# A four-layer graph network on one core: row transposes as fp32r, reordered evictions, and six small loads on another queue

## The chip, the cores and the metric

One core of a Trainium2 chip. The metric is the device time of one launch, in microseconds, as the median of three runs. TensorE does the matrix products and writes to PSUM banks; VectorE and ScalarE read those banks; GpSimd works on SBUF only; the queues of SyncE and ScalarE issue DMAs.

## The reference

16 graphs of 1024 nodes with 256 features, and a dense matrix of 1024 x 1024 per graph. Four layers, each `x = layernorm(x + layer(x))`, all in float32:

- layer 0: five small graph convolutions over groups of the first 25 nodes of each graph;
- layer 1: attention, `softmax over (leaky(ai + aj) where adj > 0, and a sink)` times `z = x W + bW`, with `ai` and `aj` a dot product of `z` per node;
- layer 2: `relu(((1 + eps) x + adj x) W1 + b1) W2 + b2`, hidden width 512;
- layer 3: `silu(rmsnorm((eps x + adj x) W1 + b1)) W2 + b2`, hidden width 1024.

## The kernel before, in words

A prologue computes layer 0 for all graphs at once (lines 113 to 654), and the scores of graph 0; then one loop over the 16 graphs does layers 1 to 3. Products are made from high and low parts: `hi` is the fp32r rounding of a value and `lo` what is left, and three matmuls (hi hi, hi lo, lo hi) make one product. The order on each engine is written out by hand in one function per engine (`graph`), and semaphores tie the engines. Graph b+1's scores and attention are prepared inside graph b.

TensorE's order in graph b (function `graph` in the tensor block):

1. aggregation of layer 1, node columns 0 to 511 (half 0), k = 0 to 7: `agg_step`, six matmuls of 128x512 each (L950, L951, L954); with it the end of layer 3 of graph b-1;
2. half 1, k = 0 to 7; behind most steps `turn_col(k, h)`, four transposes (L915) of a tile of the adjacency's columns into one of two turn banks (banks 4 and 5, taken in turn); behind k = 2 `attention_out(b, 0)` (L980, 24 matmuls);
3. aggregation of layer 2: half 0, k = 0 to 3, with `attention_out(b, 1)` behind k = 1 and `turn_col(3, 1)`, `(4, 1)`, `(5, 1)` behind k = 1, 2, 3; half 1, k = 0 to 3, with `turn_col(6, 1)` and `(7, 1)`; then k = 4 to 7 of both halves, with `aj_rows` (L928: eight transposes of a broadcast column of `aj`, the row of scores) behind k = 6 of half 1;
4. layer 2's hidden tiles (`hidden_tile`, six matmuls, L1000, L1001, L1005) and second products (L1015, fp32), for half 0 and then half 1. Hidden tile n uses bank n mod 2 and waits until tile n-2 was read;
5. aggregation of layer 3; hidden tiles of layer 3, half 0 (m = 0 to 7), with `turn_att(b+1, k)` (L901: eight transposes of an attention tile, four into each turn bank) behind m = 0, m = 4 and m = 7; the end of half 1's aggregation around `rms_sum` (L1047); `rms_row` (L1059, four transposes of a broadcast column of `rms`); `turn_att(b+1, 3)`; then hidden tiles of half 1, each with the second product of half 0 (L1029, L1033).

Who empties the banks:

- ScalarE reads a turn bank into `mt_hi` (`turn_hi`, L1163, both halves of an attention tile; `turn_col_hi`, L1174), VectorE then writes `mt_lo` (`turn_lo`, L1497; `turn_col_lo`, L1503) and frees the bank.
- `relu(b, h, m)` (L1227, ScalarE) empties a hidden bank of layer 2; `leaky` (L1210) and `exp` (L1215) are the scores of graph b+1, and `score_mask` (L1579) and `scores` (L1585) are VectorE's part of them.
- `square(b, h, m)` (ScalarE, two instructions, L1237 and L1246) empties a hidden bank of layer 3, and `add_square` (VectorE, L1611) sums the squares.
- `statistics` (VectorE, L1543 and after), a power on GpSimd (L1375), `normalize` (VectorE, L1558), `x_high` (ScalarE, L1201), `x_low` (GpSimd, L1380) turn a residual sum (`residual`, L1526 and L1531) into the next layer's operands. `agg_hi` (ScalarE, L1191) and `agg_lo` (VectorE, L1515) make `a_hi` and `a_lo` from an aggregation bank.

In the prologue ScalarE's queue issues 17 DMAs (L232 to L251) ahead of its first computation, `fus_e` (L254), which VectorE waits for (L408) before it empties the banks with the transposed adjacency (`AT`, L456); ScalarE copies those side by side (`AT_side`, L265) in 28 pieces; TensorE's L580 waits for the last. SyncE's queue issues the graphs, layer 0's weights, x, four weight matrices (L215 to L218; VectorE's L415 waits for all four) and eight adjacency rows (L220).

Of the kernel before, what the change touches and what calls it, by code (L numbers as in the profile page):

```python
# [46 lines left out]
def adj_resnorm(nc, x, adj, L0_W1, L0_b1, L0_W2, L0_b2, L0_fusion_w, W, bW, wai, bai, waj, baj,  # L47
# [3 lines left out]
    with ExitStack() as ctx:  # L51
# [41 lines left out]
        ai, aj = sb("ai", [P, NT]), sb("aj", [P, NT])  # L93
# [5 lines left out]
        graph0 = (att, att_r, ident_r, x_even, sq_sum, stat0, mv0, ve, rstd, qi, qj, ai, aj)  # L99
# [14 lines left out]
def prologue(nc, ctx, sem, banks, ident, ones, WT_hi, WT_lo, W12, W12_hi, W12_lo, W13, W13_hi, W13_lo,  # L114
# [4 lines left out]
    att, att_r, ident_r, x_even, sq_sum, stat0, mv0, ve, rstd, qi, qj, ai, aj = graph0  # L119
# [6 lines left out]
    with ExitStack() as pro:  # L126
# [70 lines left out]
        with nc.Block() as block:  # L197
            @block.sync
            def _(sp):
# [30 lines left out]
            def _(act):  # L230
                with nc.allow_non_contiguous_dma(reason="small columns"):
# [13 lines left out]
                    for dst, src in ((b12[:], L2_b1.rearrange("(t p) -> p t", p=P)),  # L245
                                     (b13[:], L3_b1.rearrange("(t p) -> p t", p=P)),
                                     (rms_col[:], rms_w.rearrange("(t p) -> p t", p=P)),
                                     (bW_row[:], row(bW).to_broadcast([P, D])),
                                     (b22_row[:], row(L2_b2).to_broadcast([P, D])),
                                     (b23_row[:], row(L3_b2).to_broadcast([P, D]))):  # L250
                        act.dma_start(dst, src).then_inc(s_bload, 16)  # L251
# [4 lines left out]
                for g in range(NG):  # L256
# [5 lines left out]
                    for first, run in GROUP_RUNS[g]:  # L262
                        src = AT[:, g].rearrange("p t (b j) -> p t b j", j=PAD)
                        for t in range(T0):
                            last = nc.scalar.activation(cols[:, t, :, at:at + run], src[:, t, :, first:first + run], ACT.Copy)  # L265
                        at += run
# [390 lines left out]
def layers(nc, sb, sem, banks, ident, ones, WT_hi, WT_lo, W12_hi, W12_lo, W13_hi, W13_lo,  # L657
# [5 lines left out]
    att, att_r, ident_r, x_even, sq_sum, stat0, mv0, ve, rstd, qi, qj, ai, aj = graph0  # L663
# [33 lines left out]
    ms, rms = sb("ms", [P, 2, 4]), sb("rms", [P, 2, 4])  # L697
# [118 lines left out]
    with nc.Block() as block:  # L816
# [74 lines left out]
        def _(pe):  # L891
# [29 lines left out]
            def aj_rows(b, first):  # L921
                pe.wait_ge(s_aj, b + 1)
                for i in range(2):
                    if not first:
                        turn_free(i, turn_aj_use(b))
                    for j in HALF_TILES:
                        t = 4 * i + j
                        mm = nc.tensor.transpose(turn_bank[i][:, j * P:(j + 1) * P],  # L928
                                                 aj[:, t:t + 1].to_broadcast([P, P]), ident[:])
# [121 lines left out]
            def rms_row(b, h):  # L1051
# [107 lines left out]
        def _(act):  # L1159
            def turn_hi(b, k):  # L1160
                for i in range(2):
# [96 lines left out]
            def graph(b, buf, first, last):  # L1258
# [233 lines left out]
        def _(dve):  # L1492
            def turn_lo(b, k):
                for i in range(2):
# [135 lines left out]
            def graph(b, buf, first, last):  # L1630
# [165 lines left out]
```

## Time and profile before

| | |
|---|---|
| median of 3 runs | 2726.66 us (2725.57 to 2726.69) |
| the profiled execution | 2724.53 us, span 2722.7 us |
| granted TensorE clock, mean over the span | 0.984 |
| prologue, up to the first `aj_rows` | 97.4 us |
| one graph, from `aj_rows` to `aj_rows`, 1156.00 to 1316.88 | 160.9 us |
| TensorE busy in that graph | 158.8 us, granted clock 1.00 |
| VectorE, ScalarE, GpSimd busy in it | 124.9, 96.1, 78.5 us |

A row of a timeline reads: start, time from the start of the first to the end of the last of the instructions that are merged in it, engine, line, operation, output<-inputs, shape, count, and in brackets the idle time of the engine before it and what ended it. Matmuls are pipelined, so rows of TensorE overlap; the distance from one start to the next is what a matmul costs in a stream.

### The profile page before, as it was taken

What the parts mean: (1) busy time and instruction counts of PE and PEld (TensorE: products, weight loads), DVE (VectorE), ACT (ScalarE), POOL (GpSimd) and SP (SyncE); (2) the same over time, 40 slices, a digit from 0 to 9 for tenths busy, and PEclk for the clock granted to TensorE, in tenths of its full rate; (3) what the DMA queues carried; (4) which work ended last, traced back from release to release, by engine and by line L of the source; (5) the groups of instructions that cost most, each with busy time, mean ns of one, the idle gap of its engine ahead of it and who ended that gap; (6) DMA issues with size and microseconds to landing.
All of it is one profiled execution on the core that took longest, in us unless ns stands there. A gap on an engine that the chain in (4) does not pass through costs nothing.

```text
span 2722.7 us, 41123 instructions
## 1 busy us (share of the span) xinstructions
PE 2608.1 (96%) x14650; PEld 2229.5 (82%) x14650; DVE 2030.3 (75%) x4504; ACT 1557.8 (57%) x2911; POOL 1274.9 (47%) x1385
## 2 busy tenths in 40 slices
PE   6499999999999999999999999999999999999997
PEld 5478888888888888888888888888888888888886
DVE  5776877868787786868878686886878778687735
ACT  2546557564755756466575646656475675647524
POOL 2243554535455454545535454553535555354533
PEclk8699999999999999999999999999999999999998
DMA  7040402204040220403013040311304022040200
GB/s 227 20 126 1 155 1 82 74 10 146 1 147 10 77 79 1 155 1 122 34 47 109 1 155 1 95 61 30 126 1 155 1 86 71 12 144 1 78 1 16
DMA packets 205224, 181.00 MB, mean 66 GB/s; under 512 B 17367, under 2 KB 186718, under 8 KB 205022
## 3 DMA queue, kind: packets, MB, share of 16 engines
q1 hardware_dynamic: 197454, 177.04, 20.4%
q10 hardware_dynamic: 7568, 1.34, 0.4%
q8 instruction: 118, 1.93, 0.3%
q14 instruction: 84, 0.69, 0.1%
HBM read 161.15 MB, written 17.19 MB: 65 GB/s over the span
## 4 chain that ended last, share of the span: by engine, by line
PE 68%; DVE 16%; ACT 8%; issue 4%; POOL 1%; ACTq 0%; DVEq 0%; POOLq 0%
PE bank L950 10%; PE bank L954 9%; PE bank L951 9%; PE bank L1015 8%; PE bank L1000 6%; PE bank L1001 6%; PE bank L1005 6%; PE bank L1029 5%; PE bank L901 3%; DVE stat L1543 3%; PE bank L1033 2%; DVE x_odd L1558 2%; DVE x_even L1558 2%; DVE hid L1627 2%; ACT hid L1251 2%
## 5 line engine op out<-in xcount | busy, mean ns | idle before, releaser
L950 PE MATMUL bank<-mt_hi,x_hi 128*128 128x512 f32 x1536 | 627.5, 409 | 0.8 <-ACT x_hi L1201 0.7
L954 PE MATMUL bank<-mt_hi,x_lo 128*128 128x512 f32 x1536 | 602.2, 392 | 0.0
L951 PE MATMUL bank<-mt_lo,x_hi 128*128 128x512 f32 x1536 | 601.1, 391 | 0.0
L1375 POOL TENSOR_TENSOR rstd<-ve,neg_half 128x4 f32<-128x4 f32 x126 | 161.3, 1280 | 416.0 <-DVE ve L1551 415.6
L954 PEld LDWEIGHTS bank<-mt_hi,x_lo 128*128 128x128 f32 x1536 | 289.2, 188 | 62.9 <-POOL x_lo L1380 0.2
L950 PEld LDWEIGHTS bank<-mt_hi,x_hi 128*128 128x128 f32 x1536 | 289.3, 188 | 56.8 <-ACT scratch L1246 6.6
L951 PEld LDWEIGHTS bank<-mt_lo,x_hi 128*128 128x128 f32 x1536 | 290.2, 189 | 49.5
L1000 PE MATMUL bank<-a_hi,W_lo 128*128 128x512 f32 x768 | 316.8, 412 | 3.7 <-ACT hid L1227 2.9
L1611 DVE TENSOR_TENSOR sq_sum<-sq_sum,scratch 128x512 f32<-128x512 f32 x224 | 154.9, 691 | 216.0 <-ACT scratch L1246 216.0
L1001 PE MATMUL bank<-a_hi,W_hi 128*128 128x512 f32 x768 | 301.7, 393 | 0.0
L1029 PE MATMUL bank<-W_hi,hid_hi 128*128 128x256 f32 x1024 | 263.0, 290 | 19.8 <-ACT hid_hi L1256 19.8
L1174 ACT ACTIVATE mt_hi<-bank 128x512 fp32r<-128x512 f32 x256 | 153.0, 598 | 221.3 <-PE bank L915 221.3
L1029 PE MATMUL bank<-W_lo,hid_hi 128*128 128x256 f32 x1024 | 257.2, 284 | 0.0
L1237 ACT ACTIVATE hid<-bank,b 128x512 f32<-128x512 f32 x256 | 176.7, 690 | 133.5 <-PE bank L1033 77.5
L1515 DVE TENSOR_TENSOR a_lo<-bank,a_hi 128x512 fp32r<-128x512 f32 x192 | 126.2, 685 | 162.9 <-ACT a_hi L1191 162.7
L1251 ACT ACTIVATE hid<-hid 128x512 f32<-128x512 f32 x256 | 161.2, 630 | 146.3 <-DVE hid L1627 144.7
L1005 PE MATMUL bank<-a_lo,W_hi 128*128 128x512 f32 x768 | 237.9, 391 | 0.0
L1380 POOL TENSOR_TENSOR x_lo<-x_even,x_hi 128x256 fp32r<-128x256 f32 x192 | 162.7, 862 | 143.8 <-ACT x_hi L1201 143.8
L1503 DVE TENSOR_TENSOR mt_lo<-bank,mt_hi 128x512 fp32r<-128x512 f32 x256 | 173.1, 685 | 72.3 <-ACT mt_hi L1174 72.0
L1015 PE MATMUL bank<-W,hid 128*128 128x256 f32 x1024 | 226.2, 379 | 0.0
L1191 ACT ACTIVATE a_hi<-bank 128x512 fp32r<-128x512 f32 x192 | 109.0, 593 | 201.1 <-PE bank L954 197.1
L1029 PEld LDWEIGHTS bank<-W_hi,hid_hi 128*128 128x128 f32 x1024 | 195.2, 191 | 31.9 <-issue 26.6
(169 smaller groups left out, 5978.1 us busy)
## 6 DMA issues: line engine op xcount, KB each, us to landing
att<-in_adj SPq DMA_DIRECT2D x128, 512.0 KB, 8.1
adj_col<-in_adj SPq DMA_DIRECT2D x256, 256.0 KB, 3.0
out<-x_even SPq DMA_DIRECT2D x64, 128.0 KB, 2.9
out<-x_odd SPq DMA_DIRECT2D x64, 128.0 KB, 2.7
x_odd<-in_x SPq DMA_DIRECT2D x56, 128.0 KB, 4.2
x_even<-in_x SPq DMA_DIRECT2D x49, 128.0 KB, 3.8
G<-in_L_gnn_W SPq DMA_DIRECT2D x2, 2048.0 KB, 19.0
W_raw<-in_L_gnn_W SPq DMA_DIRECT2D x2, 1024.0 KB, 10.5
```

Source lines behind the costliest of these rows:

```text
L950: nc.tensor.matmul(dst[:], hi, mt_hi[:, k, cols], start=k == 0, stop=False)
L951: nc.tensor.matmul(dst[:], hi, mt_lo[:, k, cols], start=False, stop=False)
L954: mm = nc.tensor.matmul(dst[:], lo, mt_hi[:, k, cols], start=False, stop=done)
L1000: nc.tensor.matmul(dst, w_lo[:, d, cols], a_hi[:, d, :], start=d == 0, stop=False)
L1001: nc.tensor.matmul(dst, w_hi[:, d, cols], a_hi[:, d, :], start=False, stop=False)
L1005: mm = nc.tensor.matmul(dst, w_hi[:, d, cols], a_lo[:, d, :], start=False, stop=d == DT - 1)
L1015: mm = nc.tensor.matmul(out_bank[t // 2][:, t % 2 * D:(t % 2 + 1) * D], src[:, t * P:(t + 1) * P], W22[:, m, :], start=(m == 0 and t % 2 = ...
L1029: nc.tensor.matmul(out_bank[t // 2][:, t % 2 * D:(t % 2 + 1) * D], hi[:, t * P:(t + 1) * P], r[:, m, :], start=(m == 0 and t % 2 == 0 and ...
L1237: nc.scalar.activation(hid[:, m, :], src, ACT.Identity, bias=b13[:, m:m + 1])
L1251: nc.scalar.activation(h_m, h_m, ACT.Silu).then_inc(s_silu, 1)
L1380: nc.gpsimd.tensor_tensor(x_lo[:, t, :], x_bufs[buf][:, t, :], x_hi[:, t, :].bitcast(F32), ALU.subtract).then_inc(s_x_lo, 1)
L1503: nc.vector.tensor_tensor(mt_lo[:, k, cols], turn_bank[i][:], mt_hi[:, k, cols].bitcast(F32), ALU.subtract).then_inc(s_turn_free[i], 1)
```

## The change

- `aj_r` and `rms_r` are fp32r names for the memory of `aj` and `rms`; `aj_rows` and `rms_row` transpose these with `ident_r`, instead of the fp32 tiles with `ident`.
- ScalarE, layer 2: `relu(b, 0, m)` for m = 1, 2, 3 moves ahead of `leaky(b+1, m-1)`.
- VectorE, layer 1: `turn_col_lo(b, 4, 0)` moves ahead of `statistics(b+1, 0, 0)`; `turn_col_lo(b, 3, 1)` moves ahead of `residual(b, 1, 1)`.
- Layer 3, half 0: the two halves of attention tiles 0 and 1 are evicted apart: ScalarE's half 0 behind `square` 0 (and 4), half 1 behind `square` 1 (and 5); VectorE's half 0 behind `add_square` 1 (and 5), half 1 behind `add_square` 2 (and 6).
- TensorE: `turn_att(b+1, 3)` moves from ahead of hidden tile 0 of half 1 to behind it.
- Prologue: six loads of bias columns and rows move from ScalarE's queue to the end of SyncE's loads; the 28 copies of `AT_side` become 7, each over all four tiles.

```diff
+        with ExitStack() as place:
+            aj_r = sb("aj_r", [P, NT], F32R, place)
+        aj, ai = sb("aj", [P, NT]), sb("ai", [P, NT])
...
                 for t in range(NT):
                     sp.dma_start(att[:, t, :], adj[0, t * P:(t + 1) * P, :]).then_inc(s_att_in[t], 16)
+                with nc.allow_non_contiguous_dma(reason="small columns"):
+                    for dst, src in ((b12[:], ...), (b13[:], ...), (rms_col[:], ...),
+                                     (bW_row[:], ...), (b22_row[:], ...), (b23_row[:], ...)):
+                        sp.dma_start(dst, src).then_inc(s_bload, 16)
                 sp.wait_ge(s_bload, 16 * 6)
...
-                    for dst, src in ((b12[:], ...), ...):
-                        act.dma_start(dst, src).then_inc(s_bload, 16)
...
-                        for t in range(T0):
-                            last = nc.scalar.activation(cols[:, t, :, at:at + run], src[:, t, :, first:first + run], ACT.Copy)
+                        last = nc.scalar.activation(cols[:, :, :, at:at + run], src[:, :, :, first:first + run], ACT.Copy)
...
-                        mm = nc.tensor.transpose(turn_bank[i][:, j * P:(j + 1) * P],
-                                                 aj[:, t:t + 1].to_broadcast([P, P]), ident[:])
+                        mm = nc.tensor.transpose(turn_bank[i][:, j * P:(j + 1) * P].bitcast(F32R),
+                                                 aj_r[:, t:t + 1].to_broadcast([P, P]), ident_r[:])
...
-                    mm = nc.tensor.transpose(row_bank[:, j * P:(j + 1) * P],
-                                             rms[:, h, j:j + 1].to_broadcast([P, P]), ident[:])
+                    mm = nc.tensor.transpose(row_bank[:, j * P:(j + 1) * P].bitcast(F32R),
+                                             rms_r[:, h, j:j + 1].to_broadcast([P, P]), ident_r[:])
...
                 rms_row(b, 0)
-                if not last:
-                    turn_att(b + 1, 3)
                 for m in range(HT3):
                     hidden_tile(b, 3, 1, m)
+                    if not last and m == 0:
+                        turn_att(b + 1, 3)
...
                 diag_hi(b, 1)
+                relu(b, 0, 1)
                 if not last:
                     leaky(b + 1, 0)
-                relu(b, 0, 1)
+                relu(b, 0, 2)
                 if not last:
                     leaky(b + 1, 1)
-                relu(b, 0, 2)
+                relu(b, 0, 3)
                 if not last:
                     leaky(b + 1, 2)
-                relu(b, 0, 3)
-                if not last:
                     exp(b + 1, 0)
...
                     square(b, 0, m)
-                    if not last and m in (0, 4):
-                        turn_hi(b + 1, m // 4)
+                    if not last and m % 4 < 2:
+                        turn_hi(b + 1, m // 4, (m % 4,))
...
                 turn_col_lo(b, 3, 0)
+                turn_col_lo(b, 4, 0)
                 if not last:
                     statistics(b + 1, 0, 0, 1 - buf)
-                turn_col_lo(b, 4, 0)
                 turn_col_lo(b, 5, 0)
...
+                turn_col_lo(b, 3, 1)
                 residual(b, 1, 1, buf)
-                turn_col_lo(b, 3, 1)
                 turn_col_lo(b, 4, 1)
...
                     add_square(b, 0, m)
-                    if not last and m in (1, 5):
-                        turn_lo(b + 1, m // 4)
+                    if not last and m % 4 in (1, 2):
+                        turn_lo(b + 1, m // 4, (m % 4 - 1,))
```

## Rows read from the trace of the kernel before

**Rows 1.** The page, its first part: busy time and share of the span by engine.

```profile
PE 2608.1 (96%) x14650; PEld 2229.5 (82%) x14650; DVE 2030.3 (75%) x4504; ACT 1557.8 (57%) x2911; POOL 1274.9 (47%) x1385
```

**Rows 2.** Timeline of TensorE, layer 3 of a graph from the middle.

```profile
1210.45 0.80 PE L901 MATMUL bank<-ident_r,att_r 128*128 128x128 f32 x8
...
1212.08 0.62 PE L1005 MATMUL bank<-a_lo,W_hi 128*128 128x512 f32 x2
...
1214.10 0.50 PE L1000 MATMUL bank<-a_hi,W_lo 128*128 128x512 f32 x1
...
1215.60 0.97 PE L901 MATMUL bank<-ident_r,att_r 128*128 128x128 f32 x8
...
1223.94 0.35 PE L1029 MATMUL bank<-W_hi,hid_hi 128*128 128x256 f32 x1 [0.94 <-ACT hid_hi L1256]
```

**Rows 3.** Timeline of ScalarE, the squares of hidden tiles 5 and 6.

```profile
1212.76 0.71 ACT L1237 ACTIVATE hid<-bank,b 128x512 f32<-128x512 f32 x1
1213.33 0.71 ACT L1246 ACTIVATE scratch<-bank,b 128x512 f32<-128x512 f32 x1
1214.10 0.69 ACT L1237 ACTIVATE hid<-bank,b 128x512 f32<-128x512 f32 x1
```

**Rows 4.** Timeline of VectorE, the low parts of attention tile 1.

```profile
1214.69 1.28 DVE L1497 TENSOR_TENSOR mt_lo<-bank,mt_hi 128x512 fp32r<-128x512 f32 x2
```

**Rows 5.** Timeline of VectorE, layers 1 and 2 of the next graph.

```profile
1273.74 1.40 DVE L1543 BATCH_NORM_STATS2 stat<-x_even 128x6 f32<-128x256 f32 x4
...
1275.66 1.28 DVE L1503 TENSOR_TENSOR mt_lo<-bank,mt_hi 128x512 fp32r<-128x512 f32 x2
...
1292.13 1.28 DVE L1515 TENSOR_TENSOR a_lo<-bank,a_hi 128x512 fp32r<-128x512 f32 x2
...
1298.31 1.66 DVE L1526 SCALAR_TENSOR_TENSOR x_odd<-bank,rden,x_odd 128x256 f32<-128x256 f32 x4
...
1303.01 0.69 DVE L1503 TENSOR_TENSOR mt_lo<-bank,mt_hi 128x512 fp32r<-128x512 f32 x1
```

**Rows 6.** Timelines of ScalarE and of GpSimd, the same stretch.

```profile
1273.77 0.61 ACT L1174 ACTIVATE mt_hi<-bank 128x512 fp32r<-128x512 f32 x1
...
1306.78 2.98 POOL L1380 TENSOR_TENSOR x_lo<-x_odd,x_hi 128x256 fp32r<-128x256 f32 x4
```

**Rows 7.** Timeline of TensorE, the same stretch and its `aj_rows`.

```profile
1276.49 0.51 PE L915 MATMUL bank<-ident_r,mt_lo 128*128 128x128 f32 x4 [0.20 <-DVE mt_lo L1503]
...
1293.62 0.28 PE L980 MATMUL bank<-WT_hi,a_hi 128*128 128x256 f32 x1
...
1300.71 0.52 PE L915 MATMUL bank<-ident_r,mt_lo 128*128 128x128 f32 x4 [0.54 <-DVE mt_lo L1503]
...
1304.26 0.46 PE L915 MATMUL bank<-ident_r,mt_lo 128*128 128x128 f32 x4
...
1316.88 1.04 PE L928 MATMUL bank<-ident,aj 128*128 128x128 f32 x8
```

**Rows 8.** Timelines of ScalarE and TensorE, layer 2's hidden tiles.

```profile
1322.85 0.67 ACT L1227 ACTIVATE hid<-bank,b 128x512 f32<-128x512 f32 x1
...
1333.92 0.67 ACT L1227 ACTIVATE hid<-bank,b 128x512 f32<-128x512 f32 x1
...
1323.57 0.50 PE L1000 MATMUL bank<-a_hi,W_lo 128*128 128x512 f32 x1 [0.19 <-ACT hid L1227]
...
1334.70 0.43 PE L1000 MATMUL bank<-a_hi,W_lo 128*128 128x512 f32 x1
```

**Rows 9.** Timelines of ScalarE (and its queue), TensorE and VectorE in the prologue.

```profile
16.59 2.91 ACTq L251 DMA_DIRECT2D b<-in_L_gnn_b  x2
...
29.59 1.28 ACT L254 ACT_TABLE_LOAD   x1 [29.59 <-issue]
...
36.43 4.65 PE L580 MATMUL bank<-AT_side,X 128*128 128x212 f32 x16 [6.89 <-ACT AT_side L265]
...
49.50 0.69 DVE L415 CAST W_hi<-W_raw 128x1024 fp32r<-128x1024 f32 x1 [4.39 <-DMA W<-in_L_gnn_W]
```

More of the change, by code:

```diff
@@ L92, in adj_resnorm @@
         qi, qj = sb("qi", [P, NT]), sb("qj", [P, NT])
-        ai, aj = sb("ai", [P, NT]), sb("aj", [P, NT])
+        with ExitStack() as place:
+            aj_r = sb("aj_r", [P, NT], F32R, place)
+        aj, ai = sb("aj", [P, NT]), sb("ai", [P, NT])
         s_att_in = [sem(f"adj_rows_loaded{t}") for t in range(NT)]
@@ L98, in adj_resnorm @@
         s_l0_stored = sem("layer0_stored")
-        graph0 = (att, att_r, ident_r, x_even, sq_sum, stat0, mv0, ve, rstd, qi, qj, ai, aj)
+        graph0 = (att, att_r, ident_r, aj_r, x_even, sq_sum, stat0, mv0, ve, rstd, qi, qj, ai, aj)
         graph0_sems = (s_att_in, s_stats0, s_aggr0, s_var0, s_rstd0, s_y0, s_sums, s_ai, s_aj, s_l0_stored)
@@ L118, in prologue @@
              eps2, L2_W1, L2_b1, L2_W2, L2_b2, eps3, L3_W1, L3_b1, rms_w, L3_W2, L3_b2, x_l0):
-    att, att_r, ident_r, x_even, sq_sum, stat0, mv0, ve, rstd, qi, qj, ai, aj = graph0
+    att, att_r, ident_r, aj_r, x_even, sq_sum, stat0, mv0, ve, rstd, qi, qj, ai, aj = graph0
     s_att_in, s_stats0, s_aggr0, s_var0, s_rstd0, s_y0, s_sums, s_ai, s_aj, s_l0_stored = graph0_sems
@@ L220, in _ @@
                     sp.dma_start(att[:, t, :], adj[0, t * P:(t + 1) * P, :]).then_inc(s_att_in[t], 16)
+                with nc.allow_non_contiguous_dma(reason="small columns"):
+                    for dst, src in ((b12[:], L2_b1.rearrange("(t p) -> p t", p=P)),
+                                     (b13[:], L3_b1.rearrange("(t p) -> p t", p=P)),
+                                     (rms_col[:], rms_w.rearrange("(t p) -> p t", p=P)),
+                                     (bW_row[:], row(bW).to_broadcast([P, D])),
+                                     (b22_row[:], row(L2_b2).to_broadcast([P, D])),
+                                     (b23_row[:], row(L3_b2).to_broadcast([P, D]))):
+                        sp.dma_start(dst, src).then_inc(s_bload, 16)
                 sp.wait_ge(s_bload, 16 * 6)
@@ L244, in _ @@
                        .then_inc(s_gbload, 16)
[L245 to L250, printed above, removed]
-                        act.dma_start(dst, src).then_inc(s_bload, 16)
                 act.wait_ge(s_dve, 5)
@@ L659, in layers @@
            cI2, gapI, neg_half, graph0, graph0_sems, x, adj, x_l0, out):
-    att, att_r, ident_r, x_even, sq_sum, stat0, mv0, ve, rstd, qi, qj, ai, aj = graph0
+    att, att_r, ident_r, aj_r, x_even, sq_sum, stat0, mv0, ve, rstd, qi, qj, ai, aj = graph0
     s_att_in, s_stats0, s_aggr0, s_var0, s_rstd0, s_y0, s_sums, s_ai, s_aj, s_l0_stored = graph0_sems
@@ L696, in layers @@
     den, rden, covered = sb("den", [P, NT]), sb("rden", [P, NT]), sb("covered", [P, NT])
-    ms, rms = sb("ms", [P, 2, 4]), sb("rms", [P, 2, 4])
+    with ExitStack() as place:
+        rms_r = sb("rms_r", [P, 2, 4], F32R, place)
+    rms, ms = sb("rms", [P, 2, 4]), sb("ms", [P, 2, 4])
     mvs = [mv0, mv, mv, mv3]
@@ L1159, in _, with turn_hi @@
         def _(act):
-            def turn_hi(b, k):
-                for i in range(2):
+            def turn_hi(b, k, halves=range(2)):
+                for i in halves:
                     act.wait_ge(s_turned[i], turn_att_use(b, k) + 1)
@@ L1492, in _, with turn_lo @@
         def _(dve):
-            def turn_lo(b, k):
-                for i in range(2):
+            def turn_lo(b, k, halves=range(2)):
+                for i in halves:
                     dve.wait_ge(s_turn_hi[i], hi_use(b, k) + 1)
```

## The prediction

> **What bounds the kernel now.** I read the page first: TensorE is busy 96% of the span [rows 1], so a shorter wait elsewhere is worth nothing unless TensorE waits for it. Then TensorE's own timeline over one graph, start to start. In a stream a 512-column matmul starts 0.23 us after the one before; wherever the distance is larger, TensorE waited. The graph has few such places, and nearly all repeat to 0.01 us in every graph, so one graph can be worked out and multiplied by 15 (in the last graph nothing is prepared for a next one). What the reader is to see in the other groups is how late the other engines are at these places: in layer 3's hidden tiles TensorE waits for the square of the tile two before [rows 2, 3], in layers 1 and 2 VectorE works nearly without a pause from 1273 to 1312 and TensorE waits for its low parts [rows 5, 7], in layer 2's hidden tiles for a relu [rows 8]. The prologue (97 us) is serial.
>
> **1. Attention tiles 0 and 1, evictions split.** Before, ScalarE has finished both halves when tile 5's bank is full: tile 5's last matmuls start at 1212.08, and the square begins at 1212.76 [rows 2, 3], when the bank is done (1212.08 + 0.62 = 1212.70). So the pair of evictions delays no square; TensorE's own transposes cover it. The square ends at 1213.33 + 0.71 = 1214.04 and tile 7 starts at 1214.10: this wait is the loop bank, square, bank, and the split does not shorten it. After, half 1 (0.48 us from start to start; two take 1.08) stands between the squares of tiles 5 and 6. ScalarE is free at 1213.33 + 0.57 = 1213.90, then at 1214.38, so square 6 starts at 1214.38 instead of 1214.10 [rows 3] and ends 1.25 later, at 1215.63. VectorE has `add_square(6)` ahead of its own half 1: 0.61 for the sum, 0.69 for the low part, so the bank is free at about 1216.97. Before, both low parts ran 1214.69 to 1215.97 [rows 4]. TensorE wants half 1 of the turn banks for `turn_att(b+1, 2)` four transposes after 1215.60, at 1215.92 [rows 2]; it would wait to 1217.02, that is 1.10, of which 0.17 is waited already (0.97 for these eight against 0.80 for the eight at 1210.45 [rows 2]). Net +0.93. The same at tiles 1 and 2 puts square 2 later by 0.26 and tile 4 behind it; TensorE had 0.1 to 0.2 of room there: 0 to 0.28, I take 0.2. Nothing behind it can take the 1.1 back, since rms, `a_hi`, `a_lo`, the first scaling and silu all hang on the aggregation that follows. Sum +1.13 a graph, x 15 = **+17.0**.
>
> **2. `turn_att(b+1, 3)` behind a hidden tile, and `rms_row` as fp32r.** The second product at 1223.94 waits 0.94 for ScalarE's `hid_hi` [rows 2], a chain from the aggregation's end; the hidden tile, the transposes and the row all lie in its shadow, in either order, with 0.9 us to spare. A shorter row makes that wait longer. The other `rms_row` (half 1) is followed by waits on the same kind of chain. **0**, bounds -0.1 and 0 a row; without the cover the row would give 0.1.
>
> **3. `aj_rows` as fp32r.** Eight fp32 transposes take 1.04 us [rows 7], eight fp32r ones 0.80 [rows 2]: -0.24, in a stretch where TensorE waits for nothing, and the relu chain behind starts earlier too. x 15 = **-3.6** (bounds -4 and -2, since these rows hold the end of the last transpose as well). The Trainium skill, "FP8 and Floating Point Precision", section "TensorE Precision Notes", says that true FP32 takes four passes; by it the row transposes would fall to a quarter, -0.78 a graph and -12 in all. The rows speak against that for transposes: the difference is 1.3 times.
>
> **4. Low part of column tile 4 ahead of the statistics.** It stood behind them at 1275.66 [rows 5], and TensorE waited 0.20 idle (0.37 start to start, with 0.06 for the cold start of the stream) for it at 1276.49 [rows 7]. After, TensorE gains 0.42. But VectorE does the statistics at 1273.74 in the order of before [rows 5], and tile 4's high part is at ScalarE only from 1273.77 to 1274.38 [rows 6]. VectorE stands still for 0.68 and all that follows on it is 0.68 later: through the residuals, three statistics and three normalizations to `a_lo`, 1292.13 to 1293.41 [rows 5], which ends at 1294.09 instead. `attention_out(b, 1)` needs it and starts at 1293.62 [rows 7], 0.2 after it is there. TensorE, though early, then starts at about 1294.15 and starts cold: +0.6 against before. The gain is gone and 0.6 is lost.
>
> **5. Low part of tile (3, 1) ahead of the residual.** The residual's four instructions start at 1298.31 and take 1.66 [rows 5]; TensorE waits 0.54 idle (0.71, and 0.06 more) at 1300.71 [rows 7]. After, the low part is there about 1299.7 even with VectorE 0.68 late: -0.77. Next is tile (5, 1), at VectorE from 1303.01 to 1303.70 [rows 5], after to 1304.38; TensorE wants the bank at 1304.26 [rows 7], after at about 1304.1: +0.35. Then GpSimd's `x_lo` of tile 4, whose power waits for VectorE's statistics: 1306.78 + 0.74 [rows 6], after 1308.2, wanted at 1308.0: +0.3. Parts 4 and 5 together, +0.6 - 0.77 + 0.35 + 0.3 = +0.5, in graphs 1 to 14: **+7.0**. (In 3 of these 14 the wait at 1300.71 isn't there and the +0.6 stands alone.) Bounds: -1.2 a graph if VectorE's pause does not pass on, +0.9 if nothing of -0.77 is kept.
>
> **6. Relus ahead of leaky.** Tile 3 waits for relu 1, 1322.85 to 1323.52, and starts at 1323.57 [rows 8]: 0.46 with the restart. After, relu 1 starts about 1322.06 and that wait goes. But `leaky` 0 is then 0.7 later, the scores and mask 2 behind it too, and `leaky` 2, which waited for mask 2, becomes the last before `exp` 0: ScalarE comes to `exp` 0 at the same time. From there it has no pause up to relu (1, 0), 1333.92 to 1334.59, and hidden tile (1, 2) starts at 1334.70 [rows 8], which is just then. TensorE comes 0.46 earlier and waits for it. **0**, bounds -0.46 and +0.15 a graph.
>
> **7. Prologue.** ScalarE's queue issues the six loads from 16.59 to 29.6, and its first computation is at 29.59 for that reason alone [rows 9]. After, it can start at 17; VectorE has the transposed blocks out at about 30.3, when TensorE's L570 is done; seven copies instead of 28 end at 30.8, and L580, at 36.43 [rows 9], starts at about 30.9: -5.6. What is late next: VectorE's split of the weights, 49.50, waits for the last weight load [rows 9]. The six loads no longer compete with it (their packets are about 4 us of the 16 engines' time), so it lands at about 46; if it does not, 1 to 4 us of the 5.6 are lost. SyncE issues the six behind the adjacency rows, at 47 or earlier; they are needed only at the prologue's end. `aj_rows(0)` stands on the chain: -0.7 by part 3 at half clock. I take **-6.0**, bounds -7 and -2. The Trainium skill, "Trainium Kernel Development and Optimization", "Key Constraints", has it that another issuing queue saves only issue time; here that is the 13 us of rows 9, and the earlier landing would come from the order in the queue.
>
> **Sum.** 17.0 + 7.0 - 3.6 - 6.0 = +14.4 on the profiled execution's 2724.5, 2739; the median of the runs stands 2.1 above it: **2741 us**. A measurement of this kernel tells 0.2% (5.4 us) from no change.
>
> **Rivals.**
> (a) *TensorE keeps every wait that the change removes* (faster). Place: the low parts of parts 4 and 5; price -0.42 and -0.77; it decides if VectorE's pause of 0.68 closes before `a_lo`. For it: VectorE is busy 75% only [rows 1]. Against: the stretch is contiguous. With part 1 as worked out, 14.4 - 7.0 - 14 = -7: about 2720. Chance 0.12.
> (b) *The split costs nothing either* (much faster): the half-1 low part is in time for `turn_att(b+1, 2)`, and the relus' 0.46 and the 0.3 before tiles 3 and 7 are gained as well. It decides if half 1 is free by 1215.9. Against: `add_square(6)` needs square 6, which cannot end before 1215.36 even unslipped. 2720 - 17 - 16 = 2687. Chance 0.08.
> (c) *The split costs half*, because the waits ahead of tile 4 and in parts 4 and 5 are smaller than by my rows: 2726 to 2732, within 0.2% or just above. Chance 0.10.
> (d) *The late VectorE costs a second place too*, such as `aj` or `a_lo` of half 0: 2753 or more. Chance 0.06.
> (e) *fp32 transposes take four times the passes of fp32r ones*: a row would fall from 1.04 to 0.26, 2741 - 12 + 4 = 2733. Against: 1.04 and 0.80 [rows 7, 2]. Chance 0.02.
> The forecast, 2734 to 2753: 0.62. That the fp32r names change nothing on TensorE (the transposes cost the same) only takes the 3.6 back: 2745, inside it.
>
> **How the numbers follow.** Faster: (a) + (b) = 0.20. Same: (c) = 0.10. Slower: forecast + (d) + (e) = 0.70. The range holds the forecast, (c) and most of (a): 2713 to 2753; the forecast's own is 2734 to 2753.
>
> **What would show it.** In the new profile: `turn_att(b+1, 2)` shows an idle of about 1 us on TensorE, released by VectorE's `mt_lo`; VectorE has a 0.6 pause before its low part of column tile 4; the first L980 of half 1 waits for `a_lo`; relu 1 releases nothing, relu (1, 0) does; L580 starts near 31 and the first `aj_rows` near 91.7; a graph takes 162.4 instead of 160.9. It is wrong if `turn_att(b+1, 2)` runs through, or if a graph is shorter than 160.9.

## The result, and the profile after

The changed kernel takes **2759.9 us** (median of 4 runs, 2758.1 to 2760.8), the kernel before 2726.1 (4 runs): a ratio of 1.0123, 95% interval 1.0111 to 1.0135. It is slower by 33.8 us. The prediction had the sign right and the size wrong: 2741 was forecast, and the range ended at 2753.

| us, profiled executions | before | after | |
|---|---|---|---|
| time | 2724.5 | 2760.3 | +35.8 |
| span | 2722.7 | 2758.5 | +35.8 |
| first `aj_rows` (prologue) | 97.36 | 92.04 | -5.3 |
| 15 intervals from `aj_rows` to `aj_rows` | 2346.0 | 2385.2 | +39.2 |
| last `aj_rows` to the end | 279.3 | 281.2 | +1.9 |
| the interval shown, graph 7 | 160.9 | 163.4 | +2.5 |
| granted TensorE clock | 0.984 | 0.985 | |

The clock is the same, and so is the work. First the page of the kernel after, which answers to [rows 1]: TensorE's busy time is only 12 us longer, the span 36 us, so most of the loss is waiting.

```profile
PE 2620.5 (95%) x14650; PEld 2218.4 (80%) x14650; DVE 2035.2 (74%) x4504; ACT 1563.4 (57%) x2887; POOL 1259.3 (46%) x1385
```

The line numbers are 4 or 5 higher than before. TensorE's timeline of the kernel after, at the places of [rows 2, 7, 8]:

```profile
1187.28 0.50 PE L1004 MATMUL bank<-a_hi,W_lo 128*128 128x512 f32 x1 [0.65 <-ACT hid L1232]
...
1229.30 0.47 PE L905 MATMUL bank<-ident_r,att_r 128*128 128x128 f32 x4
1230.78 0.53 PE L905 MATMUL bank<-ident_r,att_r 128*128 128x128 f32 x4 [1.01 <-DVE mt_lo L1502]
...
1308.85 0.39 PE L984 MATMUL bank<-WT_hi,a_hi 128*128 128x256 f32 x1 [0.43 <-DVE a_lo L1520]
...
1319.41 0.51 PE L919 MATMUL bank<-ident_r,mt_lo 128*128 128x128 f32 x4 [0.42 <-DVE mt_lo L1508]
```

The brackets give the idle time only. After a pause the next matmuls also start further apart than in a stream: the one behind L984 at 1308.85 follows after 0.22, in the kernel before after 0.12. The losses below include this restart. The four waits together are more than what a graph loses, since other waits are gone. The second is the one that was forecast for the split: `turn_att(b+1, 2)` has its first four transposes at 1229.30 and its last four 1.48 later. The third and the fourth (the transposes of column tile (7, 1)) are VectorE late by its pause. The first is hidden tile (1, 2) of layer 2, and it was not forecast. The two waits of before that the change aimed at (0.20 and 0.54 idle [rows 7]) and tile 3's (0.19 idle [rows 8]) are gone.

VectorE's timeline of the kernel after, for the second and the third wait, which answers to [rows 4, 5]:

```profile
1228.40 0.68 DVE L1502 TENSOR_TENSOR mt_lo<-bank,mt_hi 128x512 fp32r<-128x512 f32 x1
1229.44 0.69 DVE L1616 TENSOR_TENSOR sq_sum<-sq_sum,scratch 128x512 f32<-128x512 f32 x1 [0.35 <-ACT scratch L1251]
1230.05 0.68 DVE L1502 TENSOR_TENSOR mt_lo<-bank,mt_hi 128x512 fp32r<-128x512 f32 x1
...
1289.02 0.69 DVE L1508 TENSOR_TENSOR mt_lo<-bank,mt_hi 128x512 fp32r<-128x512 f32 x1 [0.59 <-ACT mt_hi L1179]
1289.63 1.40 DVE L1548 BATCH_NORM_STATS2 stat<-x_even 128x6 f32<-128x256 f32 x4
...
1307.52 1.28 DVE L1520 TENSOR_TENSOR a_lo<-bank,a_hi 128x512 fp32r<-128x512 f32 x2
```

The second half of attention tile 1 (half 1) stands behind `add_square(6)`, which stands still for square 6: the bank is free at 1230.73, and TensorE goes on at 1230.78. Below it, VectorE pauses 0.59 for the high part of column tile (4, 0), and `a_lo` ends at 1308.80, where TensorE's L984 waits for it.

ScalarE's timeline in layer 2's hidden tiles, the kernel before:

```profile
1160.93 1.14 ACT L1210 ACTIVATE att<-aj_row,ai 128x1024 f32<-128x1024 f32 x1
...
1164.68 1.15 ACT L1210 ACTIVATE att<-aj_row,ai 128x1024 f32<-128x1024 f32 x1 [0.41 <-DVE scratch L1579]
...
1166.42 1.28 ACT L1215 ACT_TABLE_LOAD   x1
...
1173.03 0.69 ACT L1227 ACTIVATE hid<-bank,b 128x512 f32<-128x512 f32 x1
```

and the kernel after:

```profile
1174.49 1.15 ACT L1215 ACTIVATE att<-aj_row,ai 128x1024 f32<-128x1024 f32 x1
...
1178.78 1.15 ACT L1215 ACTIVATE att<-aj_row,ai 128x1024 f32<-128x1024 f32 x1 [0.95 <-DVE scratch L1584]
1179.94 1.28 ACT L1220 ACT_TABLE_LOAD   x1
...
1186.56 1.25 ACT L1232 ACTIVATE hid<-bank,b 128x512 f32<-128x512 f32 x2
```

Count from each graph's `aj_rows` (1156.00 before, 1168.93 after). `leaky` 0 starts at 4.93 and 5.56, `leaky` 2 at 8.68 and 9.85, the table load of `exp` 0 at 10.42 and 11.01, relu (1, 0) at 17.03 and 17.63. So `leaky` 0 is 0.63 late, `leaky` 2 is 1.17 late, and of that 0.6 is left from `exp` 0 on, for ScalarE has no pause behind it in either kernel. TensorE, 0.7 earlier, waits 0.40 at tile (1, 0), whose low part comes from an `agg_hi` behind `exp` 0, and 0.88 ahead of tile (1, 2).

Why `leaky` 2 is later than `leaky` 0 shows in the scores between them, `scores` 0 on VectorE and the four bias adds on GpSimd. The kernel before:

```profile
1162.22 1.28 DVE L1585 CUSTOM_DVE_ANT_0 att<-att,scratch 128x1024 f32<-128x1024 f32 x1 [1.98 <-ACT att L1210]
```

```profile
1162.37 5.66 POOL L1386 TENSOR_TENSOR x_even<-x_even,b_row 128x256 f32<-128x256 f32 x4
```

and the kernel after:

```profile
1175.78 1.83 DVE L1590 CUSTOM_DVE_ANT_0 att<-att,scratch 128x1024 f32<-128x1024 f32 x1 [3.22 <-ACT att L1215]
```

```profile
1175.08 4.24 POOL L1391 TENSOR_TENSOR x_even<-x_even,b_row 128x256 f32<-128x256 f32 x4
```

Before, the scores start 0.15 ahead of the adds; after, they start 0.70 behind the first of them and take 0.55 longer.

The prologue in the kernel after, ScalarE, TensorE and VectorE, which answers to [rows 9]:

```profile
17.11 1.28 ACT L257 ACT_TABLE_LOAD   x1 [17.11 <-issue]
...
31.51 3.13 PE L582 MATMUL bank<-AT_side,X 128*128 128x212 f32 x16 [1.21 <-ACT AT_side L267]
...
92.04 1.23 PE L932 MATMUL bank<-ident_r,aj_r 128*128 128x128 f32 x8 [8.79 <-PEq L199]
...
46.10 0.69 DVE L417 CAST W_hi<-W_raw 128x1024 fp32r<-128x1024 f32 x1 [4.74 <-DMA W<-in_L_gnn_W]
```

ScalarE's first work starts 12.5 us earlier, TensorE's L582 4.9, VectorE's split of the weights 3.4, and the first `aj_rows` 5.3.

### The profile page after: what moved, and what is told of

The parts are those of the page before. It is cut to its first block, busy times and chain, and to the rows that moved or that the text cites. A ratio compares the mean times of both kernels' runs of the same rounds, so it can differ in the third digit from the quotient of the medians.

```text
span 2758.5 us, 41114 instructions
## 1 busy us (share of the span) xinstructions
PE 2620.5 (95%) x14650; PEld 2218.4 (80%) x14650; DVE 2035.2 (74%) x4504; ACT 1563.4 (57%) x2887; POOL 1259.3 (46%) x1385
## 4 chain that ended last, share of the span: by engine, by line
PE 55%; DVE 22%; ACT 13%; issue 5%; POOL 1%; DVEq 0%; ACTq 0%; POOLq 0%
PE bank L954 8%; PE bank L958 8%; PE bank L955 8%; PE bank L1004 5%; PE bank L1033 5%; PE bank L1005 5%; PE bank L1009 5%; PE bank L1019 4%; DVE stat L1548 4%; PE bank L905 3%; DVE x_even L1563 3%; DVE x_odd L1563 2%; PE bank L1037 2%; DVE hid L1632 2%; ACT att L1215 2%
## 5 line engine op out<-in xcount | busy, mean ns | idle before, releaser
L1256 ACT ACTIVATE hid<-hid 128x512 f32<-128x512 f32 x256 | 161.2, 630 | 145.6 <-DVE hid L1632 143.9
L1590 DVE CUSTOM_DVE_ANT_0 att<-att,scratch 128x1024 f32<-128x1024 f32 x128 | 187.4, 1464 | 52.3 <-ACT att L1215 51.7
```

Of the source, the lines that this page charges most:

```text
L1590: nc.vector.tensor_tensor_reduce(out=own, in0=own, in1=masks[t % 2][:], scale=1.0, scalar=-3.0e38, op0=ALU.add, op1=ALU.max, accum_out=top ...
```

## The experiments

Every run but the last changes the kernel before. To read them, the span is cut at the first and the last `aj_rows`. The first one stands between 97.4 and 100.4 us in runs whose prologue is that of before, so the prologue alone moves a single run by 3 us. The loop (15 intervals, 2346.0 us before) shows a part's effect more sharply than the time does, and both are given. A loop is read from one profiled execution; "graph 7" is the interval of the rows above, compared place by place with the kernel before.

**1. The relus alone.** Order on ScalarE: relu 1, `leaky` 0, relu 2, `leaky` 1, relu 3, `leaky` 2.

```diff
-                if not last:
-                    leaky(b + 1, 0)
                 relu(b, 0, 1)
+                if not last:
+                    leaky(b + 1, 0)
...
```

> Only the order of the three relus and leakys is changed from the kernel before. Theory: TensorE gains the 0.48 us of tile 3, but leaky 0 is 0.63 late, the scores and mask 2 behind it 1.2 late, so exp 0, agg_hi (2,1) and relu (1,0) come 0.6 late on ScalarE, and TensorE waits 0.4 at hidden tile (1,0) and 0.8 ahead of tile (1,2): +0.8 a graph, about 2726 + 12 = 2738. Rival (my forecast): the gain is only used up at tile (1,2), 2726. Second rival: the 0.8 needs the other parts of the change, and the relus alone gain their 0.46: 2719.

Measured: 2736.8 us, ratio 1.0040 (1.0025 to 1.0054); loop +10.4. In graph 7: -0.48 at tiles 2 and 3, +0.40 at tile (1, 0), +0.88 ahead of (1, 2). The first theory holds; the relus need no other part of the change to lose.

**2. The split alone.** ScalarE's half 1 of attention tiles 0 and 1 behind square 1 (5), VectorE's behind `add_square` 2 (6), as in the change.

```diff
-                    if not last and m in (1, 5):
-                        turn_lo(b + 1, m // 4)
+                    if not last and m % 4 in (1, 2):
+                        turn_lo(b + 1, m // 4, (m % 4 - 1,))
```

> Only the split of the evictions of attention tiles 0 and 1 is changed from the kernel before. Theory: turn_att(b+1, 2) waits 1.0 us more for VectorE's low part of half 1, tile 4 0.1 to 0.2 more: +1.1 to +1.3 a graph, 2743 to 2745. Rival: the wait is made up in the chain behind it (rms, scaling, silu), 2726 to 2733.

Measured: 2744.1 us, ratio 1.0062 (1.0047 to 1.0077); loop +16.8, graph 7 +0.23 ahead of tiles 3 to 5 and +1.05 at `turn_att(b+1, 2)`.

**3. The low part of column tile (4, 0) alone.**

```diff
+                turn_col_lo(b, 4, 0)
                 if not last:
                     statistics(b + 1, 0, 0, 1 - buf)
-                turn_col_lo(b, 4, 0)
```

> Only VectorE's low part of column tile (4,0) is moved ahead of the statistics. Theory: TensorE gains 0.42 at tile (4,0), VectorE stands 0.68 us, and attention_out(b, 1) waits for a_lo: +0.7, with the tile behind (2,1) 0.4 and tile (3,1) later still: +0.6 to +1.0 a graph, 2735 to 2741. Rival: VectorE's pause closes ahead of a_lo and TensorE keeps its 0.42: 2720.

Measured: 2742.0 us, ratio 1.0057 (1.0042 to 1.0072); loop +18.0. In graph 7: -0.42, then +0.38 ahead of the transposes of tile (2, 1), +0.68 at `attention_out(b, 1)`, +0.29 more ahead of those of tile (5, 1): +1.07 at the end of the graph, a little over the +1.0 that was expected at most. The first interval is 1.7 longer too. By the loop it is the dearest part of the change.

**4. The low part of column tile (3, 1) alone.**

```diff
+                turn_col_lo(b, 3, 1)
                 residual(b, 1, 1, buf)
-                turn_col_lo(b, 3, 1)
```

> Only VectorE's low part of column tile (3,1) is moved ahead of the residual. Theory: TensorE gains the 0.77 us wait and, with VectorE not late as in the whole change, gives back at most 0.3 at tiles (5,1) and x_lo of tile 4: -0.4 to -0.7 in 12 graphs, 2718 to 2721. Rival: the residual 0.69 later holds statistics and x of tiles 4 to 7, and all of it comes back: 2726.

Measured: 2726.5 us, ratio 1.0000 (0.9990 to 1.0009); loop -0.1. My theory missed: the part gives nothing. Of the intervals behind the first, 10 take 160.8 to 161.1 and 4 take 160.1 to 160.2; before, 11 take 160.9 to 161.0 and 3 take 160.0 to 160.1. Graph 8 of this run, one of the long ones, TensorE:

```profile
1463.92 0.45 PE L915 MATMUL bank<-ident_r,mt_lo 128*128 128x128 f32 x4
...
1466.08 0.51 PE L915 MATMUL bank<-ident_r,mt_lo 128*128 128x128 f32 x4 [0.26 <-DVE mt_lo L1503]
```

The transposes of tile (6, 1), and of (5, 1) before them, don't wait any more, but those of (7, 1) do, for the low part of (5, 1), and of the 0.84 gained at the first place 0.46 is lost there and 0.22 more just behind it: most of the wait is only handed on. So something in front of both places takes 0.8 us in some graphs. VectorE and GpSimd of the kernel before, graph 7, in one fence each:

```profile
1295.93 1.39 DVE L1566 SCALAR_TENSOR_TENSOR sq_sum<-x_even,v_rows 128x256 f32<-128x256 f32 x1
...
1297.37 0.42 DVE L1566 SCALAR_TENSOR_TENSOR sq_sum<-x_even,v_rows 128x256 f32<-128x256 f32 x1
```

```profile
1295.57 1.48 POOL L1412 TENSOR_TENSOR hid<-hid,gapI 128x512 f32<-128x512 f32 x1
```

A dot product of `attention_sums` that takes 0.42 alone takes 1.39 when it starts 0.36 behind GpSimd's `diag_gap(b, 0)`. This is so in all 11 long graphs of before. In the three short ones the last adjacency column arrives later, `diag_gap` starts when the last dot product is already running or done, and no dot product takes over 0.71. One such graph, VectorE and GpSimd:

```profile
975.96 0.56 DVE L1566 SCALAR_TENSOR_TENSOR sq_sum<-x_even,v_rows 128x256 f32<-128x256 f32 x1
...
976.56 1.66 DVE L1526 SCALAR_TENSOR_TENSOR x_odd<-bank,rden,x_odd 128x256 f32<-128x256 f32 x4
```

```profile
976.19 1.48 POOL L1412 TENSOR_TENSOR hid<-hid,gapI 128x512 f32<-128x512 f32 x1
```

The residual, which reads one operand from PSUM, takes 1.66 beside `diag_gap` as it does in [rows 5] without it.

In experiment 3, in experiment 9 and in the kernel after, one dot product takes 1.38 to 1.40 in all 14 graphs behind the first. The three short graphs of before are gone there, which is about 2.6 us of each of these loops.

**5. `diag_gap` elsewhere**, the test of that.

```diff
-                diag_gap(b, 0)
                 rstd_of(b, 1, 1)
+                diag_gap(b, 0)
```

> Only GpSimd's diag_gap(b, 0) (1.47 us over 128 x 512 in SBUF) is moved behind its rstd_of(b, 1, 1). Theory: in the graphs of 160.9 us, not in the three of 160.0, the last dot product of attention_sums(b+1, 0..3) on VectorE starts 0.36 us after diag_gap and lasts 1.39 instead of 0.42 to 0.57, and this is the whole wait of 0.77 ahead of column tile (3,1) that the low part's new place was to remove. Moved, it meets statistics alone: all 15 graphs take 160.1: 2726 - 9 = 2717. Rival: the wait is the residual's own (1.66 us), and the time stays: 2726.

Measured: 2716.5 us, ratio 0.9960 (0.9945 to 0.9975); every interval behind the first is between 160.09 and 160.22. GpSimd, VectorE and TensorE, graph 7:

```profile
1301.04 1.29 POOL L1412 TENSOR_TENSOR hid<-hid,gapI 128x512 f32<-128x512 f32 x1
```

```profile
1294.72 0.42 DVE L1566 SCALAR_TENSOR_TENSOR sq_sum<-x_even,v_rows 128x256 f32<-128x256 f32 x1
...
1295.19 1.66 DVE L1526 SCALAR_TENSOR_TENSOR x_odd<-bank,rden,x_odd 128x256 f32<-128x256 f32 x4
```

```profile
1297.80 0.46 PE L915 MATMUL bank<-ident_r,mt_lo 128*128 128x128 f32 x4
```

The wait that the change worked around was a collision, and one moved line removes it.

**6. The split with VectorE's low part first.**

```diff
+                    if not last and m % 4 == 2:
+                        turn_lo(b + 1, m // 4, (1,))
                     add_square(b, 0, m)
-                    if not last and m in (1, 5):
-                        turn_lo(b + 1, m // 4)
+                    if not last and m % 4 == 1:
+                        turn_lo(b + 1, m // 4, (0,))
```

> The split as in split_only, but VectorE's low part of half 1 stands ahead of add_square 2 (and 6), not behind it. Theory: the 1.05 us at turn_att(b+1, 2) comes from the bank of half 1 being freed behind add_square(6), which itself waits for square 6; with the low part ahead of it the bank is free at about 60.1 us after aj_rows instead of 61.2 (60.0 before), so 0.2 remains there and 0.2 to 0.3 ahead of tiles 3 and 4: +0.3 to +0.5 a graph, 2731 to 2734. Rival: ScalarE's half 1 between two squares is what costs, and the wait stays: 2742 to 2745.

Measured: 2730.4 us, ratio 1.0010 (1.0001 to 1.0020); loop +4.6. TensorE's `turn_att(b+1, 2)` is whole again:

```profile
1222.91 0.96 PE L901 MATMUL bank<-ident_r,att_r 128*128 128x128 f32 x8
1223.71 0.47 PE L950 MATMUL bank<-mt_hi,x_hi 128*128 128x512 f32 x1
```

0.80 as before [rows 2]. The 1.05 us came from VectorE's order, not from ScalarE's; what is left, 0.24 ahead of tiles 3 to 5, is ScalarE's half 1 between two squares, and it buys nothing.

**7. Relus, and relu (1, 0) ahead of `leaky` 4.**

```diff
                     exp(b + 1, 1)
-                    leaky(b + 1, 4)
                 for m in range(HT2):
                     relu(b, 1, m)
+                    if m == 0 and not last:
+                        leaky(b + 1, 4)
```

> The relus as in relu_order, and relu (1,0) ahead of leaky 4 as well. Theory: the 0.82 us ahead of hidden tile (1,2) is ScalarE's order behind the late exp 0; with relu (1,0) ahead of leaky 4 it starts a leaky (1.04 us) earlier, that wait goes, and 0.40 at tile (1,0) against the 0.48 gained is left: -0.1 to +0.1 a graph, 2725 to 2728. Rival: the late scores chain shows up again at exp 2, relu (1,2) or the end of the scores, and +0.5 or more a graph stays: 2734 and above.

Measured: 2727.9 us, ratio 1.0005 (0.9995 to 1.0014). The 0.88 ahead of tile (1, 2) is gone, 0.14 is new at the tile behind it, and 0.40 at tile (1, 0) stays: graph 7 stands at +0.02 behind these tiles and at +0.08 at its end. (The loop shows +4.0; 1.7 of it is that one graph escapes the collision of experiment 4, where three did before.)

**8. Relus, and GpSimd's adds held.**

GpSimd makes the last four of its eight bias adds only when VectorE has done scores 2.

```diff
                 for t in range(NT):
+                    if t == 4 and not last:
+                        pool.wait_ge(s_top, (b + 1) * NT + 3)
                     add_bias(b, 1, t, buf)
```

> The relus as in relu_order, and GpSimd holds its bias adds of node tiles 4 to 7 until scores 2 are done, so that scores 0 to 2 do not meet them. Theory: of the 0.80 us by which exp 0 is late, 0.55 are scores 0 taking 1.83 instead of 1.28 us beside these adds; without them exp 0 is at most 0.25 late and the waits at tiles (1,0) and (1,2) shrink by at least 0.5: 0 to +0.3 a graph, 2726 to 2731. Rival: only the order on ScalarE counts, 2737 as relu_order.

Measured: 2724.8 us, ratio 0.9989 (0.9979 to 0.9998); loop -0.1. Scores 0 on VectorE, first with the relus alone, then with the adds held:

```profile
1169.57 1.82 DVE L1584 CUSTOM_DVE_ANT_0 att<-att,scratch 128x1024 f32<-128x1024 f32 x1 [2.81 <-ACT att L1210]
```

```profile
1165.30 1.23 DVE L1586 CUSTOM_DVE_ANT_0 att<-att,scratch 128x1024 f32<-128x1024 f32 x1 [2.85 <-ACT att L1210]
```

ScalarE with the adds held (`aj_rows` of this graph at 1158.25) has `exp` 0's table load at 10.29, before it 10.42:

```profile
1168.54 1.28 ACT L1215 ACT_TABLE_LOAD   x1
...
1175.15 1.32 ACT L1227 ACTIVATE hid<-bank,b 128x512 f32<-128x512 f32 x2
```

The 0.40 at tile (1, 0) is gone and 0.36 is left ahead of tile (1, 2); graph 7 ends at +0.09 instead of +0.88, although `leaky` 0 is as late as ever. So what made most of the loss was scores 0 landing in GpSimd's adds. The hold takes away more than the relus brought, though. Scores 0 take 1.23 instead of 1.83, but the mask behind them also takes 0.69 instead of 1.02, and that mask meets an add in the kernel before as well (1.04 at 1163.61). Of the 0.80 by which `exp` 0 was late, the longer scores are 0.55; the other 0.25, the late `leaky` 0 itself, is covered here by the shorter mask. The adds held without the relus had no run, so what the relus' order costs against such a kernel is not shown.

**9. Low part and high part of column tile (4, 0).** VectorE as in experiment 3, and ScalarE:

```diff
                 for k in range(2, NT):
-                    turn_col_hi(b, k, 0)
+                    if k != 4:
+                        turn_col_hi(b, k, 0)
+                    if k == 3:
+                        turn_col_hi(b, 4, 0)
```

> VectorE's low part of column tile (4,0) ahead of the statistics as in low4_only, and ScalarE's high part of it ahead of the two cover_bias in front of it. Theory: the 1.05 us of low4_only are VectorE's pause of 0.7 for the high part, which starts at 117.8 us after aj_rows behind the two; moved to 117.0, the pause is 0 and TensorE keeps its 0.42: 2726 - 5 = 2721 (2719 to 2724). Rival: the later statistics or the later covered biases (0.5 us each) make attention_out(b, 1) late all the same: 2732 or more.

Measured: 2729.9 us, ratio 1.0012 (1.0003 to 1.0022). The theory missed. VectorE (`aj_rows` of this graph at 1162.63) and TensorE:

```profile
1279.77 1.29 DVE L1506 TENSOR_TENSOR mt_lo<-bank,mt_hi 128x512 fp32r<-128x512 f32 x2 [0.76 <-ACT mt_hi L1174]
...
1298.86 1.28 DVE L1518 TENSOR_TENSOR a_lo<-bank,a_hi 128x512 fp32r<-128x512 f32 x2
```

```profile
1300.19 0.39 PE L980 MATMUL bank<-WT_hi,a_hi 128*128 128x256 f32 x1 [0.21 <-DVE a_lo L1518]
```

The pause between the two low parts is gone, and `a_lo` starts at 136.23, before at 136.13. But TensorE, 0.41 earlier, now waits for it and pays the restart: +0.48 at `attention_out(b, 1)`. TensorE had 0.2 us of room there, so a gain of 0.42 in front of it cannot be kept, with or without the pause. 0.14 more is lost at the transposes of (5, 1), and graph 7 ends at +0.21. Most of the rest of the loop's +5.7 is that no graph is short in this run (all 160.9 to 161.2), 2.6, and that the first interval is 1.4 longer.

**10. Rows as fp32r, the loads and the copies**, the three remaining parts as in the change.

```diff
-                                                 aj[:, t:t + 1].to_broadcast([P, P]), ident[:])
+                                                 aj_r[:, t:t + 1].to_broadcast([P, P]), ident_r[:])
...
-                        for t in range(T0):
-                            last = nc.scalar.activation(cols[:, t, :, at:at + run], src[:, t, :, first:first + run], ACT.Copy)
+                        last = nc.scalar.activation(cols[:, :, :, at:at + run], src[:, :, :, first:first + run], ACT.Copy)
```

> Only the fp32r rows, the six loads on SyncE's queue and the seven copies of AT_side. Theory: first aj_rows at 92.0 instead of 97.4, and 0.2 a graph less at aj_rows where the wait for the relu chain doesn't take it back: -5.4 - 3 = about 2718. Rival: TensorE, 0.2 us earlier into layer 2's hidden tiles, waits that much longer for relu 1, and only the prologue's 5.4 us are gained: 2721.

Measured: 2714.8 us, ratio 0.9955 (0.9938 to 0.9972). First `aj_rows` at 90.6, loop -1.8: graph 7 gains 0.21 at `aj_rows` and about 0.1 at each `rms_row`, loses the latter again at the waits behind them and 0.1 more in layer 3, and ends at -0.11. The time is 3 us under the 2718 that was expected, although the loop gives less than its 3: the prologue ends 1.4 earlier than expected, the stretch behind the last `aj_rows` is 1.0 shorter (278.3, before 279.3), and no cause is shown for either. Both lie within the 3 us by which single runs differ.

**11. The version that follows from this**: parts of experiment 10, the relus with both mends (7 and 8), and `diag_gap` moved; neither the split nor the low parts nor `turn_att(b+1, 3)`.

> Rows as fp32r, the prologue's loads and copies, the relus ahead of the leakys with the bias adds held and relu (1,0) ahead of leaky 4, diag_gap(b, 0) behind the power; no split, no low part moved. Theory: the parts add up: -5.4 (prologue), -3 (rows), -9 (diag_gap in 12 graphs), -0.45 x 15 = -7 (relus, whose gain is now kept): 2726 - 24 = 2702 (2699 to 2707). Rival: the gains meet in the same waits (each makes TensorE earlier at the next releaser) and at most half is kept: 2714.

Measured: **2696.8 us**, ratio 0.9890 (0.9876 to 0.9905). It is faster than both kernels, than the kernel before by 29.7 us, and 2 us under the range that was expected. The loop is shorter by 19.4. Experiments 5 and 10 give 8.4 of it to `diag_gap` and 1.8 to the rows; the other 9 is put down to the relus with both mends, a pair that had no run of its own (graph 7 gains the 0.48 at tiles 2 and 3 and gives nothing back); the first `aj_rows` stands at 90.4. The intervals behind the first are 159.31 to 159.53, and relu (1, 0) no longer holds anything:

```profile
1159.05 0.39 PE L1004 MATMUL bank<-a_hi,W_lo 128*128 128x512 f32 x1
```

**12. The whole change with all mends**, made from the kernel after: the edits of experiments 5 to 9 that are not in the change, on top of it.

> The whole change, with a mend for each place where it lost time: VectorE's low parts of half 1 ahead of add_square 2 and 6; ScalarE's high part of column tile (4,0) ahead of its two cover_bias; relu (1,0) ahead of leaky 4 and the bias adds 4 to 7 held until scores 2; diag_gap(b, 0) behind the power. Theory: nothing of the loss was any other thing, so what is left beside mended_relus_gap (2696.8) is what the split and the low parts cost once mended, 0.3 a graph for the split and 0 for the low parts: 2697 + 5 = 2702 (2700 to 2706). Rival: a part of the 34 us comes from the parts acting together and stays: 2712 or more.

Measured: 2703.3 us, ratio 0.9919 (0.9905 to 0.9932), as the theory had it. Five small moves turn the 2759.9 into this, so nothing large is left unexplained. It stands 6.5 us above experiment 11, and 3.9 in the loop: 0.2 a graph, which is the mended split of experiment 6, and 0.9 in the first interval. The low parts with their mend gain 0.42 and lose 0.47 a graph.

**The sum of the single parts.** Loops: +16.8 (split), +10.4 (relus), +18.0 (low part (4, 0)), -0.1 (low part (3, 1)), -1.8 (rows) are +43.3; the whole change shows +39.2. The parts add up but for 4 us. The loops are blurred by how many graphs escape the collision: three in the kernel before and in experiment 2, five in experiment 1, none in experiment 3 and in the kernel after. In graph 7, which is long in all of these runs, the split, the relus, the low part (4, 0) and the rows are +1.14, +0.88, +1.07 and -0.11, together +2.98, and the whole change is +2.54.

The move of `turn_att(b+1, 3)` had no run of its own. In the kernel after TensorE is 1.72 late ahead of `rms_row` and 1.70 late at the second product behind the moved transposes, so the move costs nothing there.

## Why the prediction was wrong, point by point

The forecast was +14.4, the profiled execution shows +35.8. By the prediction's own steps; "measured" is graph 7 of the kernel after, and the sums are loops of the experiments named:

| part | forecast a graph | measured a graph | us in the sum, forecast | measured |
|---|---|---|---|---|
| 1 split | +1.13 | +1.27 | +17.0 | +16.8 (experiment 2) |
| 2 `turn_att`, `rms_row` | 0 | about -0.1 | 0 | with part 3 |
| 3 `aj_rows` | -0.24 | -0.21 | -3.6 | -1.8 (experiment 10) |
| 4 and 5 low parts | +0.5 | +0.85 | +7.0 | +13.8 (what the others leave of the loop's +39.2) |
| 6 relus | 0 | +0.81 | 0 | +10.4 (experiment 1) |
| 7 prologue | | | -6.0 | -5.3 |
| behind the last `aj_rows` | | | 0 | +1.9 |

The measured column is +35.8 because its fourth row is a remainder: alone, the two low parts cost 17.9 (experiments 3 and 4). The prologue's row comes from single executions, which differ by up to 3 us. Of the 21.4 us that the forecast missed, part 6 is 10.4 and parts 4 and 5 are 6.8.

**Part 6 is the step that failed.** It said that `leaky` 2 "becomes the last before `exp` 0: ScalarE comes to `exp` 0 at the same time". The start of the chain was right: relu 1's wait goes, `leaky` 0 is 0.63 late. But I let the scores keep their 1.28 us. They start when GpSimd is in the middle of its four bias adds and take 1.83; `leaky` 2 is then 1.17 late, and relu 3, which no longer stands between it and `exp` 0, takes back 0.58 only. Experiment 8 shows it: with the adds out of the way the scores take 1.23 and `exp` 0 is on time, with the help of a mask that is shorter as well. The bound that I gave was +0.15, and +0.81 was measured. With +10.4 in place of 0 the forecast would have been 2751, and with parts 4 and 5 at +13.8 as well, 2758.

The second error is in the same part: I wrote that tile (1, 2) starts "just then" when relu (1, 0) is done, that is, with no room left, and did not carry the step on to what a late `exp` 0 would cost there, nor to the `agg_hi` ahead of it.

**Parts 4 and 5** had the mechanism right and were too small. The pause is 0.59 idle in every graph, 0.67 from start to start (forecast 0.68), and held up `a_lo`, as forecast. Mis-sized were the second places: +0.4 ahead of the transposes of column tile (2, 1), for which the text had no term, and +0.63 instead of +0.35 where the bank of tile (5, 1) is wanted. And the 0.77 of part 5 could not be kept by this move: I took the residual's 1.66 us for its cause, and it was the 1.39 us of a dot product. The three graphs in which "the wait at 1300.71 isn't there" were noticed in the prediction and not followed up, although what makes a wait come and go between equal graphs is exactly its cause. The forecast also let these three stay short; in the kernel after none is.

**Part 1** was right to 0.15 us in place, releaser and size, **part 3** to 0.03, **part 2** to 0.1, and **part 7** to 0.7, although the single executions of the prologue scatter by more. In the sum part 3 is worth half of its forecast, since later waits take some of it back (experiment 10). The signs that were named came, all but the length of a graph: the idle at `turn_att(b+1, 2)` (1.01), the pause (0.59), L980 waiting for `a_lo`, relu (1, 0) in place of relu 1, L580 near 31 (31.5) and the first `aj_rows` near 91.7 (92.0); a graph took 163.4, not 162.4. The Trainium skill's sentence on true FP32 and four passes ("FP8 and Floating Point Precision", "TensorE Precision Notes") does not hold for these transposes: eight take 0.79 from start to start in fp32 and 0.59 in fp32r, 1.3 times. Rival (e) is out. Rival (a) failed where experiment 9 shows it: even with the pause closed the room of 0.2 at `a_lo` decides. Rival (d), a second place that the late engine costs, is the one that came, in its time (2753 or more) and in that VectorE's lateness costs further places: it had 0.06, and it named VectorE and `aj` or `a_lo`, not ScalarE.

## What to carry to other kernels

Putting the work that TensorE waits for ahead of work it doesn't wait for is free only if the engine has the input by then; otherwise its whole queue slides, and the next consumers pay (experiment 3). Before a wait is worked around, compare equal iterations in which it is there and in which it isn't: here that led to one line of GpSimd worth 10 us (experiment 5). When an instruction of VectorE moves in time, look at what GpSimd does in its new place, not only at the two ends of its own chain.

## What the runs showed of the hardware

- VectorE and GpSimd block each other for whole instructions when VectorE's two inputs both lie in SBUF. A dot product of 0.42 us that starts 0.36 us behind a GpSimd add of 1.48 takes 1.39, ending 0.27 behind it. Scores of 1.23 alone take 1.82 to 1.83 beside adds, and an add of 0.74 beside them takes 1.7. Who starts first goes through: scores that start 0.15 ahead of the add take 1.28. Low parts and residuals, with one input in PSUM, take the same time in both cases (1.66 for four). The Trainium skill, "SBUF — State Buffer", "Who interferes with whom", has this rule, an exclusive lock held for the whole instruction by whoever starts first, and the trace agrees with it. The prediction did not apply it. The mask, a VectorE instruction with one input in SBUF and none in PSUM, is longer beside the adds too: 1.02 to 1.04, and 0.69 without them.
- The same collision makes a kernel with a fixed order have two lengths of a graph, 160.0 and 160.9 us, by when a DMA happens to land. Moving the add makes all graphs equal, to 0.13 us.
- Prologues of the same code ended at 97.4 to 100.4 us; the difference is 0.1% of the time of a run.
